# A new table of steps for a cross-attention, FFN and expert kernel on one core

## The reference, cut to what matters

```
x = x + xattn0(layernorm(x), ctx, ctx, mask, W, b)      # 16 heads of 16, raw ctx as keys and values, masked softmax
x = x + ffn0(layernorm(x), weight)                      # Hadamard, 4-bit rounding per token, ternary weight
x = x + xattn1(layernorm(x), ctx, bias, Wq, Wk, Wv, Wo, W1, b1, W2, b2, g1, be1, g2, be2)
                                                        # biased softmax; then h = gelu(ln(x) W1 + b1); x += h W2 + b2; layernorm
x = x + experts(x, Wr, W1, b1, W2, b2)                  # 8 experts, each takes its 512 best tokens; gelu; scatter-add
```

## Time and profile before

| | |
|---|---|
| median of three runs | 1023.83 us |
| the profiled execution's own time | 1025.06 us |
| its span | 1023.0 us |
| mean granted TensorE clock over the span | 0.921 of full speed |
| busy: PE, DVE, ACT, POOL | 84%, 66%, 38%, 45% |
| three batches in the steady part, steps 48 to 95 | 77.98, 77.98, 77.97 us |
| end of the layers (last logits read) | about 758.5 us |
| router and experts, to the end | 264.5 us |

### The profile page before, as it was taken

One profiled execution on the slowest core, in us unless ns is written; L12 is line 12 of the kernel. 1 busy time (PEld: TensorE's weight loads), 2 busy tenths in 40 slices (PEclk: granted clock), 3 DMA queues, 4 the chain that ended last, 5 costly groups with the idle time before them and its releaser, 6 DMA issues.

```text
span 1023.0 us, 18009 instructions
## 1 busy us (share of the span) xinstructions
PE 860.6 (84%) x7149; PEld 622.7 (61%) x7149; DVE 671.0 (66%) x1500; ACT 388.8 (38%) x595; POOL 461.5 (45%) x404
## 2 busy tenths in 40 slices
PE   4999977878998998999899978977723299999995
PEld 3556644455565565565565656755522289999985
DVE  3455478787798699699599477473247566666441
ACT  0222133325424524523523514432210066666662
POOL 4433435445346436436435333151221247777752
PEclk8999899999999999999999988979665589999998
DMA  5501443424434434434424334340032025555541
GB/s 187 200 24 45 191 164 130 156 98 151 154 120 149 144 115 149 139 118 146 150 80 149 131 113 174 115 145 1 21 112 73 21 64 140 148 135 133 134 74 21
DMA packets 47696, 120.57 MB, mean 118 GB/s; under 512 B 4736, under 2 KB 33920, under 8 KB 39424
## 3 DMA queue, kind: packets, MB, share of 16 engines
q1 hardware_dynamic: 41472, 111.06, 31.8%
q0 software_dynamic: 6144, 8.39, 4.6%
HBM read 111.05 MB, written 8.39 MB: 117 GB/s over the span
## 4 chain that ended last, share of the span: by engine, by line
PE 53%; DVE 28%; issue 8%; ACT 5%; POOL 2%; DMA 2%; SPq 1%; POOLq 0%; DVEq 0%; ACTq 0%
PE row_scores L434 8%; PE ps_v L522 6%; PE row_scores L1276 5%; PE ps_m L540 4%; DVE probs L675 4%; PE ps_v L1293 3%; PE ps_r L1293 3%; DVE row_scores L652 3%; DVE row_max L645 3%; PE key_scores L450 3%; PE ps_v L404 2%; PE key_scores L454 2%; DVE attnT_C L684 2%; PE ps_r L504 2%; DVE attnT_A L684 2%
## 5 line engine op out<-in xcount | busy, mean ns | idle before, releaser
L959 POOL TENSOR_TENSOR probs<-probs 128x512 f32<-128x512 f32 x128 | 162.6, 1272 | 127.0 <-ACT probs L829 65.1
L829 ACT ACTIVATE probs<-probs 128x1024 f32<-128x1024 f32 x64 | 67.6, 1057 | 257.4 <-DVE probs L675 257.3
L652 DVE CUSTOM_DVE_ANT_0 row_scores<-row_scores,bias_q 128x256 f32<-128x256 f32 x256 | 100.8, 456 | 69.6 <-PE row_scores L434 69.5
L826 ACT ACTIVATE probs<-key_scores 128x1024 f32<-128x1024 f32 x64 | 65.5, 1024 | 154.6 <-PE key_scores L450 154.6
L645 DVE TENSOR_REDUCE row_max<-row_scores 128x4 f32<-128x1024 f32 x64 | 78.1, 1221 | 44.1 <-PE row_scores L434 44.0
L675 DVE TENSOR_TENSOR probs<-key_scores,bias_k 128x1024 f32<-128x1024 f32 x64 | 77.9, 1217 | 8.1 <-PE key_scores L450 8.1
L434 PE MATMUL row_scores<-k_op_a,q_op_A 32*128 32x256 f32 x512 | 74.4, 408 | 10.3 <-DVE q_op_C L661 10.3
L434 PE MATMUL row_scores<-k_op_c,q_op_C 32*128 32x256 f32 x512 | 77.2, 421 | 5.6 <-DVE row_max L652 4.3
L450 PE MATMUL key_scores<-q_op_C,k_op_c 32*128 32x256 f32 x512 | 76.0, 416 | 0.6 <-DVE q_op_C L661 0.5
L450 PE MATMUL key_scores<-q_op_A,k_op_a 32*128 32x256 f32 x512 | 75.2, 412 | 1.1 <-DVE q_op_A L661 1.1
L1358 POOL TENSOR_TENSOR w_l<-w1e,w_h 128x512 fp32r<-128x512 f32 x32 | 52.3, 1664 | 42.0 <-ACT w_h L1309 42.0
(11 more groups left out here) (239 smaller groups left out, 2183.5 us busy)
## 6 DMA issues: line engine op xcount, KB each, us to landing
bias_q<-in_bias_q SPq DMA_DIRECT2D x32, 1024.0 KB, 4.9
bias_k<-in_bias_k SPq DMA_DIRECT2D x32, 1024.0 KB, 5.0
w1e<-in_w1e SPq DMA_DIRECT2D x8, 1024.0 KB, 5.2
w2e<-in_w2e SPq DMA_DIRECT2D x8, 1024.0 KB, 6.6
k_op_a<-in_k_a SPq DMA_DIRECT2D x32, 128.0 KB, 2.3
mask_int<-in_mask SPq DMA_DIRECT2D x8, 512.0 KB, 5.7
v_op_A<-in_v_a SPq DMA_DIRECT2D x8, 512.0 KB, 5.3
w<-in_w SPq DMA_DIRECT2D x2, 1024.0 KB, 9.2
```

What stands on the lines that cost most here:

```text
L652: ins = nc.vector.tensor_tensor_reduce(row_scores[:, j, qt * SEQ:(qt + 1) * SEQ], row_scores[:, j, qt * SEQ:(qt + 1) * SEQ], bias_q[:, m % ...
L826: nc.scalar.activation(of, key_scores[:, :, :], ACT.Exp).then_inc(exp_done, 1)
L829: nc.scalar.activation(of, of, ACT.Exp).then_inc(exp_done, 1)
L959: nc.gpsimd.tensor_tensor(both[:, :, 0, :], both[:, :, 0, :], both[:, :, 1, :], ALU.add).then_inc(blocks_summed, 1)
```

## The change

The steps of the side jobs are given anew for all four engines, and so are the exceptions for batches 0 and 4 to 7. In the steady part, `wv` goes from slot 22 to 18 (so in steps 34, 50, 66 ... right after T_A), `wo` from 36 to 35, T_B and `had` one step earlier, g0 from 43 to 42, T_R and `lg` one step earlier, `wk` from 10 to 12, and f2 is spread otherwise. VectorE's stR, apR and stA go with them. For batch 7 the chain T_B to wq comes earlier than batch 5's f1 and f2 in part, and in the last steps half of batch 6's f2 comes after batch 7's `wo`. In addition:

- A round of two quads of A alone is now an interleaved `pe_round`; only two quads of C are still apart.
- The first mask is made on VectorE (step -32), and no longer on GpSimd.
- The preparation of the ternary weight is split into four parts, one in each of steps -10 to -7; what needs it stands at step -5 instead of -6.
- ScalarE computes a small exponential of its own ahead of everything (`first_exp`).
- The useless matmuls: 28 and 24 instead of 64 at the start, 8 instead of 10 in steps -11 to 8, and 48 new ones ahead of the last T_R.
- f1_3 of batch 6 uses another bank, and a job in a borrowed bank waits for its turn there too.
- Batch 7's context is loaded one position later.

```diff
-PE_SLOT = {"wb": -6, "wa": 2, "T_A": -32, "T_B": 4, "wo": 36, "had": 5, "wv": 22, "T_F": 39, "T_q": 7, "tern": 8, "f1_0": 40,
+PE_SLOT = {"wb": -5, "wa": 0, "T_A": -32, "wv": 18, "wo": 35, "T_B": 3, "had": 4, "T_F": 39, "T_q": 6, "tern": 8, "f1_0": 40,
...
-OTHER_BANK = {("T_F", 7): "k0", ("f1_0", 7): "k1", ("f1_2", 7): "r0", ("f1_3", 7): "r1"}
+OTHER_BANK = {("f1_3", 6): "r1", ("T_F", 7): "k0", ("f1_0", 7): "k1", ("f1_2", 7): "r0", ("f1_3", 7): "r1"}
...
-            elif (job, b) in TURN:
+            if (job, b) in TURN:
...
             if job == "T_R":
+                if b == NB - 1:
+                    pe.wait_ge(max_added, 2 * len(ORDER))
+                    pe_keep_busy(48, ps_r)
...
-            pe_keep_busy(64)
+            pe_keep_busy(28, ps_m[1])
...
-                if now is not None and then is not None and now.kind == then.kind:
+                if now is not None and then is not None and now.kind == then.kind == C:
                     pe_scores_apart(pe, now, then, half)
...
-                if -10 <= step <= 16 and step not in (-6,):
-                    pe_keep_busy(10)
+                if step == -30:
+                    pe_keep_busy(24, ps_m[1])
+                if -11 <= step <= 8 and step != -5:
+                    pe_keep_busy(8, ps_m[1])
...
-            if job == "wb":
-                ve_start(ve)
+            if job[:2] == "wb":
+                ve_start(ve, int(job[2]))
+            if job == "mask":
+                ve.wait_ge(ld["mask"], 16)
+                nc.vector.tensor_scalar(mask_bf[:, 0, :, :], mask_int[:, :, :], 0, MASKED,
+                                        ALU.is_equal, ALU.mult).then_inc(S["mask_ready"], 1)
...
+            nc.scalar.activation(first_exp[:, :], half_neg[:, :], ACT.Exp)
...
-            if job == "mk":
+            if job == "mk" and b > 0:
```

## The result

The changed kernel takes 980.3 us (median of four runs, 978.26 to 980.63) against 1024.7 for the kernel before on the same chip: a ratio of 0.956, 95% interval 0.954 to 0.958. It is faster by 44 us, where 64 were forecast; 980 lies inside the range of 943 to 990, and outside the 945 to 972 that had most of the chance. The profiled execution took 980.22 us, with a span of 978.4.

A forecast was written before the change was run, and what follows sets the result against it. No engine is full, so the order of the engines' waits was taken to set the time. Savings of 8.8, 11.2, 5.2, 6.2, 10.7, 4.1 and 18 sum to 64.2: 960 us, likeliest 945 to 972, range 943 to 990.

The forecast's parts named there:

- The start: Up to step -8: first scores at 13.5 instead of 19.84 us, two row-score steps at 3.15 each; -8.8 us.
- the steady part: Three batches from step 48: fewer waits of wv and f1_2, less idle time, 74.4 us a batch; -10.7 us.
- the way to step 16: From 98.64 us to step 16: filler ends at step 8, T_C, wk, wq move earlier; 27.25 to 22, -5.2 us.
- A alone: Steps -8 to 5: interleaved rounds at 3.43 us a step plus values and side jobs, 58.8 for 70.0; -11.2 us.
- rival 1: Half of the gain comes because moved jobs find new waits: 990 us, or any part down to 972; chance 0.27.
- the rise: Steps 16 to 47: one wait of wv and some lower clock go, later steps at 4.5 us; -6.2 us.
- the end: From 572.56 us: batch 7's chain, C's steps, wo and f1 come sooner; -18 us, between -11 and -25.
- Rival 3: Slower by the clock: fewer fillers in steps -10 to 16 leave steps -8 to 31 at the lower level; 1034 us, chance 0.03.
- My own sign of being wrong: Whole kernel: the forecast would be wrong if, among other signs, the clock's low stretches grow; no size given.
- the five that I had taken off on an estimate: End of the layers: 22.9 us of gain cut to 18 in case VectorE's chain decides or the clock falls.
- the quarter of the idle time: Steady batches: a quarter of the 3.3 us idle time left goes as jobs no longer meet; -0.9 us a batch.
- The lock between VectorE and GpSimd: First steps: weight preparation might wait for GpSimd's whole mask, up to 3.65 us longer, 964 instead of 960; not counted.

The follow-up runs named there:

- my two mends: Changed kernel with more fillers and batch 0's apB later, plus batch 6's wv in step 113 and batch 4's yf one step later: ratios 0.947, 0.946; without these two 0.9445.

## Why the prediction was right, and where it was short

**The direction and most terms held.** The start (-7.8 for -8.8), the steady part (-9.4 for -10.7; the first two batches 74.28 and 74.27 for 74.4), steps 96 to 109 (-3.4 for -4.1), the way to step 16 (-4.1 for -5.2) came about as worked out, each a little short. VectorE's bound of 3.43 a step in A alone was met exactly in most steps that have no side job, and the run with the interleaved rounds alone gave 58.24 for 58.8. The value of 960 was 20 off, so the range was right by what it took in for rival 1 ("half of it comes"). Of that rival's conditions, the rise that gains little came true, and A alone (3.9 lost of its 8) and the end (3.0 of 7) in part; f1_2 waited 0.85 and not 2.0, and the start's clock was full.

**The rise was the step that failed**: -6.2 forecast, 2.0 longer measured. I counted the fillers' end at step 8 as a gain in the stretch to step 16 and nothing behind it, and took the lower clock as something that the change would lessen. Rival 3 had the mechanism (fillers taken where TensorE has the least to do) but asked for the whole stretch at the lower level. A part of it was enough: the four low stretches cost 5 of the 7.2 us by which steps 16 to 31 missed, and the fillers alone gave them back. My own sign of being wrong, low stretches that grow, came true in this stage (one of 6.8 us before, at 175.2 to 182.0; four now). The other 2.2 are missing at full clock too, and no run shows why. The sentence in rival 3 that interleaved rounds leave little idle time as in steps 32 to 109 was wrong for steps 16 to 31, where 14.7 of 72.55 us are idle; but 13.2 of 67.31 were idle before, so the sum of idle time alone does not tell when the clock falls. With the old table and the old fillers the interleaved rounds took 66.86 there, so the fall came with the new table or with the fewer fillers; which of the two is open.

**A alone was short by 3.9.** "Five with a side job of 1 to 2 us" is the term: apB of batch 0 took 2.62 behind a wait of 1.14, and the clock fell behind it. It had the slot where VectorE stands between GpSimd's reciprocal root and GpSimd's additions. The run with T_B moved shows that the wait follows apB, and with apB and the chain behind it one step later the stage came to 59.7. A smaller slip: the 61.31 us of the earlier trace rows hold 13 steps (-8 to 4), 4.7 a step, and not 14 at 4.38.

**The start** was 1.0 short: the first scores came 0.8 later than forecast, behind the fillers and not behind qA. The forecast also put the 19.84 us ahead of them at the lower clock; the trace of before has 0.96 there, and 0.51 only in the 8.81 that follow.

**The end was short by 3.0**, and by 7.9 before the five that I had taken off on an estimate. From wo on all is as forecast (6.6 for 6.1, 7.6 for 7.5). The chain to the first rows of batch 7's C took 73.7 for 70.5, with the waits of T_q, of the row scores behind it and of tern shown above, and the steps of C (ten, not the nine of the text; the sum had used ten) 54.2 for 50. By these waits it is VectorE's work, with the lower clock behind it; that is read from the rows and not tested, and my two mends did not shorten the end, so what would is open.

**The steady part came out right, and its split nearly so.** From before to after, steps 50 to 57 of a batch (wv, T_B, the rounding) fall from 39.87 to 36.76 us, 3.1 for the 1.7 and 0.9 forecast; steps 58 to 60 (gelu) from 16.08 to 14.86, 1.2 for 0.95; the others grow by 0.6. That the sum was right so owes something to the quarter of the idle time that I took without a row. The runs that move one job back do not bear these prices out as they stand: wv 7 or 21 us in all, depending on the place, gelu about 9, where the idle time priced them at 8.5 (five batches) and 5.7 (six). For gelu the difference is within the noise. For wv the rows show what comes on top: the length of the job in a full step (2.3 us), a new wait (2.09) and, in some batches, a stretch at the lower clock (1.7).

**The lock between VectorE and GpSimd**, which I set aside for the first steps, had no test there: the parts of the ternary weight of 128x256 took 0.34 and 0.35 each, but they began at 20.28 or later, when GpSimd's mask (15.76, 3.65 us) was over. It fits apB, whose two instructions end at 68.74 and 70.00, each 0.15 after a GpSimd instruction (68.59 and 69.85). Alone the same work takes 0.73, as for batch 1:

```profile
120.38 0.73 DVE L709 TENSOR_SCALAR nrm_BG<-x_all,mv_B,rstd_B 128x256 f32<-128x256 f32 x2
```

The whole trace of the changed kernel bears it out. Of L709's single instructions, the 17 that began while a GpSimd addition or subtraction of two tensors (TENSOR_TENSOR) was under way took 1.00 to 1.36 us, and every one ended 0.15 to 0.16 after it; the 69 that began with nothing under way on GpSimd took 0.39 to 0.42. Ten began in the middle of GpSimd's mask of 3.65 us, and they took 0.40 to 0.50: that instruction did not hold them up. So GpSimd's additions are what made apB long, and the two engines meet at more than semaphores here. The Trainium skill, "SBUF — State Buffer", section "SBUF: two separate sides", has it that a VectorE instruction in a two-port mode and one of GpSimd take a shared port pair in turn, each for its whole length. The 17 agree with that, the ten do not, and that L709 runs in such a mode is not shown here.

## What to carry to other kernels

Price a wait on TensorE with what follows it: here a wait of 1 to 5 us was often followed by work at half the speed (apB's 2.94, the mask's 5.07, wo's 4.05), though not each time: behind the same 0.85, f1_2 took 1.99 in one batch and 3.60 in another. Useless matmuls in a stage where TensorE stands idle can be worth several microseconds (5 here), but where TensorE then waits long anyhow they were worth nothing. A job moved out of a bank's way still needs a step with room for its own length; look at both before moving it.

## What the runs showed that I had not expected

VectorE made the mask of 128x1024 integers to bf16 in 0.66 us, half of the lower of my two bounds (1.23); GpSimd took 3.65. The same layernorm step takes 0.73 alone (batch 1) and 2.62 beside GpSimd's additions (batch 0). With the interleaved rounds alone, which take less of TensorE's time, the profiled execution had a lower clock more than ninety microseconds later, in a stage that they do not touch (0.94 instead of 0.98 in steps 32 to 47); why it fell just there stays open.
